# A decoder layer on one core: multiplications without a reader in waits of TensorE

## The reference

```python
for i in range(4):
    residual = x
    q, k, v = x @ Wq[i] + bq[i], x @ Wk[i] + bk[i], x @ Wv[i] + bv[i]
    Q, K = elu(q) + 1, elu(k) + 1
    KV = sum over tokens of K * v;  Ksum = sum over tokens of K
    V = Q * KV / (Q * Ksum + 1e-6)
    a = gelu(gelu(V @ Wo[i] + bo[i]))
    x = ln(a + residual)
    x = ln(gelu(gelu(x @ W1[i] + b1[i]) @ W2[i] + b2[i]) + x)
```

## Time and profile before

| what | before |
|---|---|
| median of 3 runs (lowest, highest) | 876.4 us (876.37 to 877.59) |
| the profiled execution, its own time | 877.94 us |
| its span, from the first to the last instruction | 876.2 us |
| mean granted clock of TensorE in the span | 0.971 |
| PE busy | 802.2 us (92%) |
| DVE busy | 686.6 us (78%) |
| ACT busy | 572.9 us (65%) |
| POOL busy | 561.5 us (64%) |

### The profile page before, as it was taken

One profiled execution on the slowest core, in us unless ns is written; L12 is line 12 of the kernel. 1 busy time (PEld: TensorE's weight loads), 2 busy tenths in 40 slices (PEclk: granted clock), 3 DMA queues, 4 the chain that ended last, 5 costly groups with the idle time before them and its releaser, 6 DMA issues.

```text
span 876.2 us, 17388 instructions
## 1 busy us (share of the span) xinstructions
PE 802.2 (92%) x5325; PEld 529.8 (60%) x5325; DVE 686.6 (78%) x2494; ACT 572.9 (65%) x1444; POOL 561.5 (64%) x638
## 2 busy tenths in 40 slices
PE   5899999999779999999979999999999898989994
PEld 2344444444456676766646676667667566888773
DVE  4788888886678988888978858985995885375786
ACT  3588778775469999999756646655654556354434
POOL 5889888887663233333477758674888888663773
PEclk9899999999959999999999999999999989999997
DMA  8300000000015011100123222221223227265112
GB/s 241 114 1 0 1 1 0 1 0 1 0 43 152 8 56 56 38 2 2 46 52 73 64 59 50 53 69 43 59 75 84 53 77 211 86 187 150 48 50 62
DMA packets 57851, 51.88 MB, mean 59 GB/s; under 512 B 11586, under 2 KB 43042, under 8 KB 57762
## 3 DMA queue, kind: packets, MB, share of 16 engines
q1 hardware_dynamic: 55394, 46.05, 19.1%
q0 software_dynamic: 2304, 4.72, 1.9%
q10 hardware_dynamic: 64, 0.02, 0.0%
HBM read 21.66 MB, written 12.32 MB: 39 GB/s over the span
## 4 chain that ended last, share of the span: by engine, by line
PE 52%; POOL 18%; DVE 14%; issue 8%; ACT 7%; DMA 0%; ACTq 0%; DVEq 0%; POOLq 0%
PE psum L2118 5%; PE psum L1947 4%; PE psum L1980 4%; POOL area L944 4%; DVE area L1436 3%; PE psum L2288 3%; PE psum L2269 3%; PE psum L2327 3%; PE psum L1964 3%; PE psum L2006 3%; POOL area L853 3%; PE psum L2305 3%; PE psum L2191 3%; PE psum L1843 2%; POOL slot_in L932 2%
## 5 line engine op out<-in xcount | busy, mean ns | idle before, releaser
L944 POOL TENSOR_TENSOR area<-area,rinv 128x512 f32<-128x512 f32 x64 | 94.2, 1472 | 64.8 <-DVE rinv L1753 64.4
L1236 ACT ACTIVATE area<-area,negmax 128x128 f32<-128x128 f32 (+1 forms) x256 | 112.8, 444 | 17.4 <-DVE negmax L1436 17.1
L1089 ACT ACTIVATE area<-area,negmax 128x256 f32<-128x256 f32 x256 | 109.0, 507 | 0.2
L1424 DVE SCALAR_TENSOR_TENSOR area<-psum,ccol,cs 128x512 f32<-128x512 f32 x128 | 89.5, 741 | 21.5 <-PE psum L1980 21.3
L1436 DVE CUSTOM_DVE_ANT_0 area<-psum,area 128x256 f32<-128x256 f32 x256 | 93.2, 420 | 13.9 <-PE psum L1932 13.5
L1436 DVE CUSTOM_DVE_ANT_0 area<-psum,maskc 128x128 f32<-128x128 f32 (+1 forms) x256 | 75.8, 352 | 11.1 <-PE psum L2006 11.1
L1947 PE MATMUL psum<-ident,area 128*128 128x128 f32 x512 | 70.3, 278 | 8.7 <-DVE area L1476 7.3
L1980 PE MATMUL psum<-area,qkw 128*128 128x512 f32 x128 | 72.4, 648 | 5.7 <-DVE area L1424 3.9
L1226 ACT ACTIVATE area<-psum 128x512 f32<-128x512 f32 x32 | 19.1, 597 | 74.0 <-PE psum L2327 69.1
L1947 PEld LDWEIGHTS psum<-ident,area 128*128 128x128 f32 x512 | 56.7, 142 | 17.8 <-issue 11.5
L2305 PEld LDWEIGHTS psum<-ident,area 128*128 128x128 f32 x384 | 45.0, 142 | 34.5 <-issue 26.4
(11 more groups left out here) (306 smaller groups left out, 2095.8 us busy)
## 6 DMA issues: line engine op xcount, KB each, us to landing
area<-area SPq DMA_DIRECT2D x256, 64.0 KB
slot_out<-area SPq DMA_DIRECT2D x17, 256.0 KB, 2.3
area<-slot_in SPq DMA_DIRECT2D x8, 512.0 KB, 4.1
slot_in<-gate SPq DMA_DIRECT2D x5, 768.0 KB, 4.6
area<-in_L_ffn_re_w SPq DMA_DIRECT2D x14, 256.0 KB, 3.7
area<-in_mask_BxSxS_ik SPq DMA_DIRECT2D x8, 256.0 KB, 3.6
area<-in_L_attn_W SPq DMA_DIRECT2D x5, 256.0 KB, 6.2
area<-in_x SPq DMA_DIRECT2D x4, 256.0 KB, 3.4
```

The costliest lines, as they stand in the source:

```text
L944: pool.tensor_tensor(p4, p4, rinv[:, u % 4, 0:4].unsqueeze(2).to_broadcast([128, 4, w]), ALU.mult)\
L1089: last = act.activation(P[:, n % 4, r, mm, :], P[:, n % 4, r, mm, :], ACT.Exp, bias=negmax[:, n % 4, r, mm:mm + 1], scale=-1.0)
L1236: last = act.activation(Pc[:, u % 4, r, mm, 0:w], Pc[:, u % 4, r, mm, 0:w], ACT.Exp, bias=negmax[:, u % 4, r, mm:mm + 1], scale=-1.0, accu ...
L1424: last = nc.vector.scalar_tensor_tensor(rp[:, w, j, :].rearrange("p (b n) -> p b n", b=2), src.rearrange("p (b n) -> p b n", b=2), ccol[:, ...
```

## The change

A new helper issues `count` matmuls whose result nobody reads, always into the same place of a bank that is free at that point. Early ones take block 0's Wq as weights and its four projection matrices as 512 moving columns (float32). Late ones take a place matrix (float32r, 512 columns) and write bank 4. They set no semaphore. There are 4 of the early kind ahead of `o` of item 0, 4 ahead of `in1` of item 0, and 19 of the late kind in the drain (3, 6, 2, 3, 2 and 3). In `o` and `in1` the wait for the input (`p_V`, `p_r1`) now comes last, so that the added matmuls stand between the wait for a free bank and the wait for the input. Nothing is removed, and the order of the other instructions is the same on all engines.

```diff
+        CLOCK_KEPT = {-6: 2, -4: 3, -1: 3}
...
+            def keep_clock(dst, count, weights, moving):
+
+                for _ in range(count):
+                    nc.tensor.matmul(dst, weights, moving, start=True, stop=True)
+
+            def keep_clock_early(dst, count):
+                keep_clock(dst, count, wqkvo[:, 0, 0, :], wqkvo[:, 0, :, :].rearrange("p j n -> p (j n)"))
+
+            def keep_clock_late(count):
+                keep_clock(bank[4], count, place[:, 0, 0, 0:128], place[:, 0, 0, :])
...
             def context_step(n):
+                if n in CLOCK_KEPT:
+                    keep_clock_late(CLOCK_KEPT[n])
...
                     if what == "o":
                         weights("Wo", n)
-                        pe.wait_ge(p_V, n + 1)
...
                         else:
                             pe.wait_ge(s_x0, NG)
+                            keep_clock_early(bank[1], 4)
+                        pe.wait_ge(p_V, n + 1)
...
                     if what == "in1":
-                        pe.wait_ge(p_r1, n + 1)
...
                         else:
                             pe.wait_ge(s_bcol, 1)
+                            keep_clock_early(bank[5], 4)
+                        pe.wait_ge(p_r1, n + 1)
...
                     if what == "in2":
+                        if n == NB - 1:
+                            keep_clock_late(3)
...
                     if what == "in":
+                        if g == NG - 2:
+                            keep_clock_late(6)
...
                     if what == "back":
+                        if g == NG - 1:
+                            keep_clock_late(2)
```

## The result

| what | before | after |
|---|---|---|
| median, timed on one chip | 876.63 us (876.37 to 877.73) | 882.15 us (879.72 to 882.47) |
| ratio, 95% interval | | 1.005 (1.0039 to 1.006) |
| the profiled execution, its own time | 877.94 us | 881.06 us |
| its span | 876.2 us | 879.2 us |
| mean granted clock of TensorE | 0.971 | 0.979 |

The changed kernel is slower by 0.5% in the ratio, and the medians lie 5.5 us apart, where I had forecast 2 us less. One of its six executions took 2681.74 us; it is outside the range shown and the ratio, and without it the median is 882.05. The changed kernel's clock is higher in the mean, as wanted, and the time is longer all the same. The first view is the same cut by stretches as the earlier trace rows, of the kernel after: busy us and instructions of PE, PEld, DVE, ACT and POOL, then the granted clock, DMA share and GB/s.

What follows compares the result with a forecast made beforehand. PE's low clock was taken to cost time only on the chain, in ramp and drain. -0.86 - 0.83 - 0.2 + 0.1 = -1.8 us, taken as -1.9 from the 876.4 median: 874.5 us, range 872.6 to 876.6.

Steps and rivals of the forecast that it cites:

- Ramp, both parts: Four matmuls ahead of `o`, four ahead of `in1` of item 0 keep the clock up: -0.86 us.
- slower rival: Ramp: clock already low when the four ahead of `o` begin; 877.0 to 878.6 us, chance 0.08.
- about nothing: Ramp gain if the clock had stayed high through `o` anyway: faster `in1` (0.46 us) less the hold.
- What is won before 33.49 stays won.: Behind the ramp: PE works without a pause worth naming until the drain, so the ramp's gain is kept.
- falls elsewhere: Clock falls later in the ramp, its gain shrinking to about 0; the drain's stays: 875.4 us, chance 0.25.
- The drain: 19 late matmuls in bank 4 keep the clock up to the first exponentials: -0.83 us, with 0.1 us cost.
- All end before the wait does: Drain: added matmuls ahead of 235.49, 239.58, 242.83 and 247.41 fit into PE's waits and cost nothing.
- With the clock kept: Drain: `rows_q1` and `in` of group 3 run at the upper clock; `in` ends at 248.65 against 249.48.
- The start of cross-attention: PE's work from 255.4 to 262.1 runs faster, but ACT is the next thing late: only -0.2 us.
- too few in the drain: Clock still falls between the drain's added matmuls; the drain gives 0 to +0.7 us: 876.1 us, chance 0.12.

Runs made afterwards that it cites:

- old_waits_drain_b: Against before: only the 19 late matmuls, waits of `o` and `in1` in the old order from item 1, second timing; ratio 1.0025 (1.0002 to 1.0047).
- after_again: The changed kernel, unchanged, timed on another chip against before; 880.31 us, ratio 1.0027 (1.0015 to 1.004).
- old_waits_all_b: Against the changed kernel: all its added matmuls, waits back in the old order from item 1, second timing; ratio to before 1.0015 (0.9991 to 1.0038).
- old_waits_ramp_c: Against before: only the eight early matmuls, waits in the old order from item 1, third timing; ratio 1.0011 (0.9988 to 1.0034).
- old_waits_ramp: Against before: only the eight early matmuls, waits in the old order from item 1, first timing; ratio 1.001 (0.9991 to 1.0029).
- old_waits_all: Against the changed kernel: all its added matmuls, waits back in the old order from item 1, first timing; ratio to before 1.0014 (0.9995 to 1.0033).
- old_waits_all_c: Against the changed kernel: all its added matmuls, waits back in the old order from item 1, third timing; 880.32 us, ratio to before 1.003.
- old_waits_ramp_b: Against before: only the eight early matmuls, waits in the old order from item 1, second timing; ratio 1.0003 (0.9977 to 1.0028).
- fill: Against the changed kernel: old order of waits from item 1, ten more added matmuls in supposed pauses; 877.41 us, ratio to before 0.9996.
- dense: Against the changed kernel: old order of waits from item 1, added matmuls in nearly every ramp and drain pause; 877.17 us, ratio to before 0.9987.
- old_waits_drain: Against before: only the 19 late matmuls, waits in the old order from item 1, first timing; ratio 1.0015 (1.0001 to 1.0028).
- before_again: The kernel before, unchanged, run again for a second trace; one execution, 877.37 us.
- old_waits_drain_c: Against before: only the 19 late matmuls, waits in the old order from item 1, third timing; ratio 1.0017 (0.9998 to 1.0036).

## Why the prediction was wrong

**Ramp, both parts.** Right where they were worked out. Eight instructions took 3.60 us, `o` started at 20.41 (20.40), `in1` at 24.70, and `o` of item 1 at 31.70 (31.7). The slower rival did not come in any trace: the clock was up at 17 us. That the gain is 0.96 us beside before, and not the "about nothing" that the prediction gives for a later fall, hangs on where before's own fall was: beside `old_waits_drain_b`, with that later fall, it is 0.17.

**"What is won before 33.49 stays won."** This step failed. I had looked for pauses behind 33.49 and not at the one that the change itself would open: the projections at 26.01 became faster (1.88 for 3.62 us), as I wrote, and left a wait of 2.27 us ahead of `back1` of item 0. Behind it the clock fell, and `o` of item 1 took 2.02 us for 1.12. Of -0.86 (measured -0.96) nothing was left at o(2), +0.02. My rival "falls elsewhere" had this price, about 0 for the ramp; it was given 0.25. Of the eight traces with exactly this ramp, four lost the gain in this way (after, `after_again`, `old_waits_all_b`, `old_waits_ramp_c`) and `old_waits_ramp` ended 1.8 us behind before; their first `o` started between 20.22 and 20.75. The three others (`old_waits_all`, `old_waits_all_c`, `old_waits_ramp_b`) started it between 20.98 and 21.41, had no fall there and were 1.05 us ahead of before. `fill` and `dense`, which put work into the pause of 2.27 us, kept the gain too.

**The exchange of the waits.** Not priced at all. The text before the prediction says that in `o` and `in1` the input's wait now comes last, for all items, and I cost only the added matmuls. It is +0.83 us of the 3.0 in the trace and +0.18% in the one set of times that can tell it (+0.04% and 0 in the two coarse ones), the one part of the result that each of the traces shows in the same size.

**The drain.** "All end before the wait does" was right, and the cost was small: with three matmuls between `back` and the second scores the first exponential came 4.96 us behind the first scores, 4.94 before (I had taken 0.1). They are not off the chain, though: that of after runs over them for 0.70 us at 255.12, and ties there with ACT, which is ready for its exponentials at the same moment. The spacing was 0.23 us, not 0.21, and 0.43 at the lower clock. "With the clock kept" failed: it fell at 245.3 and `rows_q1` and `in` ran at the low level, so -0.83 became -0.20. Where it was kept the step holds: 44.96 for 45.83 in `old_waits_drain`, -0.87, both with the fall at 211, and 43.28 for 44.18 in `old_waits_all`, -0.90, both without it.

**The start of cross-attention.** The largest error, -0.2 against +2.21. I had read rightly that ACT hides PE's low clock from 255 to 262, and drew only that little could be won there. The same rows also say that this is a good place for a low stretch, and that a change which moves it on uncovers it. Behind it PE is on the chain. In the twenty traces, from the first exponential to v0 it takes 10.1 to 10.6 us where the low clock ends by 263.0, 11.06 where it ends at 264.25, and 11.9 to 12.7 where it ends between 266.75 and 269.0. The rival "too few in the drain" had the mechanism of a fall in the drain and priced it at 0 to +0.7, because it stopped at the first exponentials.

**The range.** It ended at 876.6. The rival on the slow side rested on one point in the ramp (the clock at 17 us) and none on a fall moved to a worse place, which can be read off. By the numbers that I had, PE's 5.89 us for some 3.2 there, uncovered, cost up to 2.7 us; with nothing from ramp and drain that gives 876.4 + 2.7 = 879.1, and the exchange comes on top.

**What stays open.** The profiled execution of after, 881.06 us, is 1.1 below its median, and that of before 1.3 above its own; so of the 5.5 us between the medians the traces explain 3.0. About 1.1 us more is how before's six executions fell: four of them lie at 876.4 to 876.7, and on the two other chips of this speed its median is 877.7 and 877.8. That the rest is the same thing in other places is likely but not shown. The mean clock, which is on record for each timed execution, speaks for it: of the twelve of `after_again` the six at 0.979 took 880.9 to 882.7 us, the six from 0.983 to 0.989 took 876.9 to 879.8; of `old_waits_all_c` the six at 0.981 took 880.4 to 883.1, the six at 0.985 took 876.5 to 880.3. Four of the five of after are at 0.979. The share of the ramp and of the drain in the 0.30% is not settled. `fill`, whose trace has v4 at 285.25 in place of 288.10, gains only 0.04% in the median. Part of that is shown: before's 288.10 hold the fall at 211 (286.62 in `before_again`), 0.9 us go to its own five matmuls, and its trace (876.14 us, clock 0.992) is of one of its three fastest executions, while the eight others have 0.986 to 0.990 and take 877.2 to 878.2. Where those fell is not on record.

## What to carry to other kernels

Work without a reader that keeps the clock up must fill the pauses up to the place where PE is no longer on the chain; where it fills only some, it moves the fall, and a fall that was hidden under another engine may come out on the path. Each group must also fit into a wait that the timeline shows: five matmuls of `fill` put where PE was not waiting cost 0.9 us. So before adding any, list the low stretches, mark which are covered and by what, and price the case in which each slides to the next uncovered place. And keep such an addition from touching anything in the steady loop: an exchanged pair of waits cost 0.065 us an item here, 0.83 us in all, as much as either part of the addition was to give. One trace of each kernel could not have told this: the traces of one and the same kernel differ by up to 2.8 us in one stretch.

## What the runs showed of the hardware

**Which wait comes last matters.** With the same two waits ahead of `in1`, and the other of them over 1.2 us earlier, the transpositions began 0.05 us behind POOL's sum when the sum's wait stood first, and 0.12 us when it stood last. The exchange ahead of `o` showed no such cost. All six traces with the exchange in `in1` need 0.8 us more from o(2) to o(15) than the fourteen without.

**The clock changes at instants that do not follow the program.** In the traces of before and of after, whose item 15 lies 1 us apart, it fell at 211.0 and rose at 214.5 and at 252.0 in both. In `old_waits_drain_c` every change stands half a us ahead of that of after (210.5, 214.0, 244.75, 251.5, 258.25), though its first `o` is only 0.3 us earlier. The Trainium skill ("TensorE: Matmul & The Clock Gate", Part 1: The HAM clock gate) says that the monitor runs free and is not started by the kernel, and that the same kernel therefore shows different counts of slow matmuls from run to run; the traces agree, with 43.28 to 45.84 us for one stretch of one kernel (`old_waits_all` and `old_waits_all_c`).

**Not only long pauses.** The longest wait of PE in the 3.8 us ahead of the fall at 211.0 in before is this one of its timeline, 0.94 us, where I had aimed at those of 3.16 and 3.00:

```profile
208.09 0.66 PE L1843 MATMUL psum<-ident,ntok 128*128 128x128 f32 x4 [0.94 <-POOL ntok L747]
```

PE worked for 1.88 of 3.80 us there, and the clock fell all the same.

**A float32r matmul of 512 columns.** Two rows of PE's timeline of after, which end the series of six:

```profile
238.12 0.62 PE L1841 MATMUL psum<-place 128*128 128x512 f32 x2
238.35 0.40 PE L1841 MATMUL psum<-place 128*128 128x512 f32 x1
```

Two take 0.62 and one 0.40, so one more costs 0.22 to 0.23 us at the upper clock. Three at the lower took 1.48, 0.43 for each beside one pipeline end.

**The start differs by itself.** The first `o` lies anywhere from 20.09 to 21.41 us in these traces, in kernels with and without the change. It follows the clock at the start: the four projection instructions that begin at 8.0 us take 2.53 us in `old_waits_drain_c`, 3.16 in `before_again` and 3.78 in `old_waits_drain_b`, and the first `o` starts at 20.09, 20.67 and 21.34. When the clock first rises differs between traces of one kernel. A gain of 0.9 us in the ramp has to be measured against that.
